# Cross-attention and mixture-of-experts kernel: the sums of squares move to two fp32r matmuls of parts that GpSimd makes, and the small work of each step is dealt out anew

## The chip, the core and the metric

One core of one Trainium2 chip runs the whole kernel in one launch. The metric is the device time of an execution in microseconds. Three executions of the kernel before are known; the median is what the change is measured against.

## What is computed

```python
x = x + xattn(layernorm(x), ctx, Wq, Wk, Wv)
x = x + moe(layernorm(x), Wr, br, gate_bias, Wup, ..., Wsd, bsd)

def xattn(x, context, Wq, Wk, Wv):            # 4 batches, 512 queries, 512 keys, 32 heads of 16
    q = rmsnorm((x @ Wq.T) per head)
    k = rmsnorm((context @ Wk_rows.T) per head)
    v = context @ Wv_rows.T
    return softmax(q @ k.T / 4) @ v
# rmsnorm(t) = t * rsqrt(mean(t * t, over the 16 of a head) + 1e-6)
```

The second part, a router with the best two of seven experts and one shared expert, all 512 wide, is not touched by the change.

## The kernel before

The attention part runs first, then `att.close()` gives its memory back and the experts follow. The attention work is cut into 16 units: a unit `u` is one batch `b` and one group `g` of 128 of the 512 columns, which holds 8 heads. A unit has 8 steps: `ab` (0 or 1) picks the even or the odd heads, `mt` one of four tiles of 128 keys. In a step `s`, TensorE makes the scores of four heads for 128 keys and 512 queries (`scored`, L253), in the four banks of `scores`; ScalarE takes the exponential of all 2048 columns at once (L610) into one of the two halves of `probs`; TensorE weighs the values with them (`weighed`, L270) and gathers the result in `o_ps`. There is one `scores`, so the next scores wait for the exponential, and the weighing of a step runs behind the scores of the next.

Between `scored` and `weighed` TensorE does everything else, in an order that is written out by hand in `between(u, s)` (L372): it projects k of the unit one or two ahead into `bank_a` (`k_chunk`, 3 matmuls each, four times a unit) and q of the unit two ahead into `bank_b` (`q_passes`, 4 matmuls each, three times a unit), sums the squares of q and k per head, turns the finished output (`out_transposes`), and in some groups computes the values of the next batch (`v_all`, twelve matmuls), transposes normalised rows (`norm_transposes`, `norm2_transposes`) and the router's logits (`gates`). All matmuls of projections are fp32r, three for one product: values are split into a high part, rounded to fp32r, and what is left.

The sums, transposes and logits go through one bank, `tr`; whose turn it is is fixed by the list in `uses` (L137), and each use waits on `tr_free` for the one before it to be read out. The sum of squares is a matmul with `blocks`, a matrix of ones in blocks of 16, so that each row gets the sum of its head:

```python
nc.scalar.activation(sq[:], bank_b[:], ACT.Square).then_inc(sqq_done, 1)                      # ScalarE, L483
nc.tensor.matmul(tr[:], blocks[:], sq[:], start=True, stop=True).then_inc(tr_ready, 1)        # TensorE, L329
```

It is plain fp32. The reciprocal root is made by ScalarE as exp(-0.5 ln(sum)) (`log_q`, `root_q`), and VectorE improves it by one Newton step, for which it needs the square of the root, `r2`, that ScalarE makes too (`root2_q`, `root2_k`, L518 and L523). `r0` and `r2` serve q and k in turn. Then VectorE copies each head's columns into the stacked form that the scores read (`stack_q`, `stack_k`), in high and low parts.

ScalarE's queue is written out in `before_exp(u, s)` (L536): what it does ahead of the exponential of a step. VectorE's is `step(u, s)` (L802). GpSimd has only seven small powers (`root`, L174) and a few memsets in this part. SyncE's queue has the loads. Each of these queues runs strictly in its written order.

The start, ahead of the loop, does the same for units 0 and 1, and the values of batch 0. Here the order of TensorE is k of unit 0, the transposes, k again, `sum_k(0)`, q of unit 0, the first values, `sum_q(0)` (L425 to L446); that of VectorE `sums_k(0)`, the low part of Wv (L929, 128x2048), `first_root_k(0)`, `newton_k(0)` and on.

## Time and profile before

| | |
|---|---|
| runs of the kernel before | 1047.79, 1046.66, 1047.68 us |
| median | 1047.68 us |
| the profiled execution | 1044.39 us, span of its profile 1042.7 us |
| granted TensorE clock over the span | 0.979 |
| TensorE matmul busy | 965.7 us (93%) |
| VectorE busy | 704.6 us (68%) |
| ScalarE busy | 517.6 us (50%) |
| GpSimd busy | 103.9 us (10%) |
| the 128 exponentials of the attention | from 41.40 to 480.90 us, 1878 ns each |

Times in the views are microseconds from the start of the span. PE is TensorE's matmuls, PEld its weight loads, DVE VectorE, ACT ScalarE, POOL GpSimd. The end of a matmul row is modelled and overlaps the next, so lengths of matmuls are read from start to start. An fp32 matmul of the program stands as two rows.

### The profile page before, as it was taken

The page shows a single profiled execution, that of the slowest core. Times are in us where ns is not written, and L with a number is a line of the kernel's source. Part 1 is how long each engine was busy: PE and PEld are TensorE (multiplying, and loading weights), DVE is VectorE, ACT ScalarE, POOL GpSimd, SP SyncE. Part 2 cuts the span into 40 slices and gives each one's busy share as a digit, 9 for nine tenths or more (in the row PEclk, how much of TensorE's full clock was granted, in tenths as well). Part 3 has the DMA queues.
Part 4 walks back from the last instruction along what each step waited for, and adds up shares of the span by engine and source line. Part 5 has one row for each costly group of instructions (what it writes and reads, how often), then busy time and mean ns, then how long its engine had stood idle before and what let it go on. Part 6 is the DMA issues. An engine that isn't in the chain of part 4 may idle for free.

```text
span 1042.7 us, 17880 instructions
## 1 busy us (share of the span) xinstructions
PE 965.7 (93%) x6728; PEld 692.5 (66%) x6729; DVE 704.6 (68%) x1387; ACT 517.6 (50%) x626; POOL 103.9 (10%) x135
## 2 busy tenths in 40 slices
PE   4999999989998999976999999999999999999686
PEld 3534443355344553332998989999899999999676
DVE  6787867876687667663678866575656574765288
ACT  4487768856786668875233232242424333342121
POOL 1000000000000000001000121111010101010652
PEclk9999999999999999997899999999999999999889
DMA  9400100001000100201410044124151542421654
GB/s 342 162 1 2 41 1 1 21 2 61 2 1 21 62 1 1 102 21 41 154 69 21 22 172 181 61 90 162 55 197 50 207 179 68 172 72 60 185 188 151
DMA packets 30024, 88.64 MB, mean 85 GB/s; under 512 B 5136, under 2 KB 5136, under 8 KB 25872
## 3 DMA queue, kind: packets, MB, share of 16 engines
q1 hardware_dynamic: 23088, 65.34, 17.0%
q0 software_dynamic: 6880, 22.55, 7.1%
q8 instruction: 36, 0.59, 0.2%
q14 instruction: 20, 0.16, 0.0%
HBM read 65.33 MB, written 22.54 MB: 84 GB/s over the span
## 4 chain that ended last, share of the span: by engine, by line
PE 45%; DVE 4%; another core or an unknown queue 2%; issue 1%; DMA 1%; ACT 1%; POOL 0%; POOLq 0%; DVEq 0%; ACTq 0%
PE u_ps L1178 14%; PE z_ps L1178 14%; PE y_ps L1178 13%; PE xt_ps L1191 2%; DVE x_sb L1611 1%; DMA xg<-xn_dram,index 1%; PE z_ps L1172 0%; DVE x_lo L1388 0%; DVE u_lo L1540 0%; PE xt_ps L1204 0%; DVE g_sb L1552 0%; DVE stats L1394 0%; DVE x_sb L1571 0%; ACT u_hi L1313 0%
## 5 line engine op out<-in xcount | busy, mean ns | idle before, releaser
L610 ACT ACTIVATE probs<-scores 128x2048 f32<-128x2048 f32 x128 | 240.4, 1878 | 78.0 <-PE scores L265 76.3
L1178 PE MATMUL z_ps<-u_hi,w_sb 128*128 128x256 f32 x896 | 167.2, 284 | 2.0 <-issue 1.9
L1178 PE MATMUL u_ps<-x_hi,w_sb 128*128 128x256 f32 x896 | 164.5, 282 | 4.0 <-issue 2.4
L1313 ACT ACTIVATE u_hi<-u_ps,b_ug 128x256 fp32r<-128x256 f32 x112 | 47.0, 471 | 237.1 <-PE u_ps L1178 235.1
L1178 PE MATMUL y_ps<-w_sb,g_hi 128*128 128x512 f32 x448 | 143.7, 402 | 12.2 <-DVE g_lo L1557 8.0
L1178 PEld LDWEIGHTS u_ps<-x_hi,w_sb 128*128 128x128 f32 x896 | 139.8, 189 | 6.9 <-issue 3.7
L1178 PEld LDWEIGHTS z_ps<-u_hi,w_sb 128*128 128x128 f32 x896 | 140.3, 189 | 2.8 <-issue 2.6
L281 PE MATMUL o_ps<-probs,v_sb 128*17 128x512 f32 x1024 | 137.3, 609 | 1.0 <-ACT probs L610 1.0
L1178 PE MATMUL z_ps<-u_lo,w_sb 128*128 128x256 f32 x448 | 126.1, 281 | 0.1
L1178 PE MATMUL u_ps<-x_lo,w_sb 128*128 128x256 f32 x448 | 125.7, 280 | 0.0
L265 PEld LDWEIGHTS scores<-q_st,k_hi 32*128 32x128 f32 x512 | 25.0, 183 | 124.0 <-ACT probs L610 70.5
L1540 DVE SCALAR_TENSOR_TENSOR u_lo<-u_ps,b_ug,u_hi 128x256 fp32r<-128x256 f32 x112 | 48.8, 478 | 84.1 <-ACT u_hi L1313 83.4
L1178 PEld LDWEIGHTS y_ps<-w_sb,g_hi 128*128 128x128 f32 x448 | 83.6, 192 | 31.7 <-DVE g_lo L1557 6.8
L1326 ACT ACTIVATE s_sb<-z_ps,b_ug 128x256 f32<-128x256 f32 x112 | 47.0, 470 | 112.3 <-PE z_ps L1178 93.8
L1178 PE MATMUL y_ps<-w_sb,g_lo 128*128 128x512 f32 x224 | 89.5, 400 | 0.0
L1552 DVE SCALAR_TENSOR_TENSOR g_sb<-u_ps,b_ug,s_sb 128x256 f32<-128x256 f32 x112 | 53.8, 481 | 50.4 <-ACT s_sb L1326 44.6
L1178 PEld LDWEIGHTS u_ps<-x_lo,w_sb 128*128 128x128 f32 x448 | 84.7, 189 | 1.0
L1178 PEld LDWEIGHTS z_ps<-u_lo,w_sb 128*128 128x128 f32 x448 | 85.1, 190 | 0.0
L265 PE MATMUL scores<-q_st,k_hi 32*128 32x512 f32 x512 | 64.9, 496 | 11.0 <-ACT probs L610 9.0
L1378 DVE TENSOR_TENSOR w_sb<-w_raw,w_sb 128x2048 fp32r<-128x2048 f32 x27 | 60.5, 2284 | 0.0
L1567 DVE TENSOR_TENSOR y_sb<-y_ps,bd 128x512 f32<-128x512 f32 x56 | 36.8, 686 | 27.0 <-PE y_ps L1178 16.3
L1301 ACT ACTIVATE w_sb<-w_raw 128x2048 fp32r<-128x2048 f32 x27 | 50.9, 1923 | 2.7 <-PEq L947 2.7
(206 smaller groups left out, 1488.9 us busy)
## 6 DMA issues: line engine op xcount, KB each, us to landing
w_raw<-w_all SPq DMA_DIRECT2D x27, 1024.0 KB, 8.6
y_dram<-y_sb SPq DMA_DIRECT2D x40, 256.0 KB, 2.1
ctx_raw<-ctx_t SPq DMA_DIRECT2D x4, 1024.0 KB, 6.1
out<-x_sb SPq DMA_DIRECT2D x16, 256.0 KB
y_dram<-xt SPq DMA_DIRECT2D x1, 3584.0 KB, 20.5
x_sb<-x SPq DMA_DIRECT2D x1, 3072.0 KB, 17.5
xn_dram<-xn SPq DMA_DIRECT2D x12, 256.0 KB, 2.0
bd<-b_down SPq DMA_DIRECT2D x9, 256.0 KB, 3.3
```

The costliest lines, as they stand in the source:

```text
L265: last = nc.tensor.matmul(scores[:, j, :], part[rows, u % 2, ab, mt * P:(mt + 1) * P], q_st[rows, u % 2, ab, :], start=(part is k_hi), sto ...
L281: last = nc.tensor.matmul(o_ps[32 * j:32 * j + HD + 1, :], v_sb[b % 2][:, mt, head, :], probs[:, t % 2, j, :], start=(mt == 0), stop=(mt = ...
L610: nc.scalar.activation(probs[:, t % 2], scores[:], ACT.Exp).then_inc(p_ready, 1)
L1178: ins = nc.tensor.matmul(out_ps, stat[a], mov[b], start=(first and a + b == 0), stop=(last and a == 1), skip_group_check=True)
L1191: last = nc.tensor.transpose(xt_ps[:, b, a, h * P:(h + 1) * P], xg[:, h, c * P:(c + 1) * P], ident[:])
L1301: nc.scalar.activation(w_sb[:, par, 0, m], w_raw[:, m], ACT.Copy).then_inc(hi_done, 1)
L1313: last = nc.scalar.activation(u_hi[:, c, :], u_ps[:, b, a, :], ACT.Identity, bias=b_ug[:, par, 0, c:c + 1])
L1326: nc.scalar.activation(s_sb[:, c, :], z_ps[:, b, a, :], ACT.Silu, bias=b_ug[:, par, 1, c:c + 1]).then_inc(s_done, 1)
L1378: nc.vector.tensor_tensor(w_sb[:, par, 1, m], w_raw[:, m], w_sb[:, par, 0, m].bitcast(FP32), ALU.subtract).then_inc(lo_done, 1)
L1540: nc.vector.scalar_tensor_tensor(u_lo[:, c, :], u_ps[:, b, a, :], bias[:, c:c + 1], u_hi[:, c, :].bitcast(FP32), ALU.add, ALU.subtract)\
L1552: nc.vector.scalar_tensor_tensor(g_sb[:, c, :], u_ps[:, b, a, :], bias[:, c:c + 1], s_sb[:, c, :], ALU.add, ALU.mult).then_inc(g_done, 1)
L1567: nc.vector.tensor_tensor(y_sb[:, h, :], y_v[:, h, :], bd[:, par, :], ALU.add).then_inc(y_done, 1)
```

## The change

Five things, all in the attention part:

- The sum of squares becomes two fp32r matmuls, of `sq_hi` and `sq_lo`, with a matrix of ones `blocks_r` that is fp32r as well. GpSimd makes the two parts from `sq`: a copy and a subtraction (`square_parts`). TensorE waits for `sq_split` instead of for ScalarE's square.
- GpSimd makes `r2` in place of ScalarE, as a product. Its order is written out as a loop over the units.
- The q and k matmuls are dealt out in fours and twos, one after the other, over the eight steps (`K_TURNS`, `Q_TURNS`; in units with an early block of values q has 4, 5 and 3 in three steps). `sum_k` goes from step 2 to step 3.
- Work that follows a read-out of `bank_a` (the second block of values, the first transposes of a batch, in group 1 the k matmuls of step 6) is issued behind `weighed`, in `after(u, s)`.
- ScalarE's small operations move: `log_k` from step 3 to 4, `root_k` from 4 to 5, `square_q` from 7 to 6; the second evacuation of transposed rows goes to VectorE (`norm_both(b + 1, 1)`). VectorE's statistics, `sums_k` and `first_root_k` move along. In the start `sum_k(0)` goes behind the q matmuls.

```diff
+            def square_parts(use):
+                n = SUM_AT[use]
+                pool.wait_ge(sqk_done if use[0] == "sum_k" else sqq_done, use[1] + 1)
+                if n:
+                    pool.wait_ge(tr_ready, TR_AT[SUMS[n - 1]] + 1)
+                nc.gpsimd.tensor_copy(sq_hi[:], sq[:]).then_inc(sq_high, 1)
+                pool.wait_ge(sq_high, n + 1)
+                nc.gpsimd.tensor_tensor(sq_lo[:], sq[:], sq_hi[:].bitcast(FP32), ALU.subtract).then_inc(sq_split, 1)
+
+            def root2_q(u):
+                pool.wait_ge(rq_ready, u + 1)
+                pool.wait_ge(norm_done, 2 * u if u else 1)
+                nc.gpsimd.tensor_tensor(r2[:], r0[:], r0[:], ALU.mult).then_inc(r2q_ready, 1)
...
+            square_parts(("sum_k", 0))
+            root2_k(0)
+            square_parts(("sum_q", 0))
+            root2_q(0)
+            square_parts(("sum_q", 1))
...
+        K_TURNS = {6: (0, 4), 7: (4, 6), 0: (6, 10), 1: (10, 12)}
+        Q_TURNS = {2: (0, 4), 3: (4, 6), 4: (6, 10), 5: (10, 12)}
+        Q_TURNS_V = {3: (0, 4), 4: (4, 9), 5: (9, 12)}
...
-            def sum_k(u):
-                begin("tr", TR_AT, ("sum_k", u), tr_free)
-                pe.wait_ge(sqk_done, u + 1)
-                nc.tensor.matmul(tr[:], blocks[:], sq[:], start=True, stop=True).then_inc(tr_ready, 1)
+            def sum_up(use):
+                begin("tr", TR_AT, use, tr_free)
+                pe.wait_ge(sq_split, SUM_AT[use] + 1)
+                nc.tensor.matmul(tr[:], blocks_r[:], sq_hi[:], start=True, stop=False, skip_group_check=True)
+                nc.tensor.matmul(tr[:], blocks_r[:], sq_lo[:], start=False, stop=True, skip_group_check=True)\
+                  .then_inc(tr_ready, 1)
...
-            k_chunk(0, 2)
-            k_chunk(0, 3)
-            sum_k(0)
-            for part in range(3):
-                q_passes(0, part)
+            k_turns(0, 6, 12)
+            q_turns(0, 0, 12)
+            sum_up(("sum_k", 0))
             v_all(scores[:, 0, :], 0, 0).then_inc(first_v, 1)
-            sum_q(0)
+            sum_up(("sum_q", 0))
...
                 elif s == 3:
-                    if nxt:
-                        root2_q(u + 1)
                     if more and g == 2:
                         norm_high(b + 1, 3)
+                elif s == 4:
                     if nxt:
                         log_k(u + 1)
-                elif s == 4:
+                elif s == 5:
                     if nxt:
                         root_k(u + 1)
-                elif s == 5:
                     group_out(u, 0)
                 elif s == 6:
                     if more and g == 1:
                         norm_high(b + 1, 0)
-                    if nxt:
-                        root2_k(u + 1)
-                else:
-                    if more and g == 1:
-                        norm_high(b + 1, 1)
                     if u + 2 < UNITS:
                         square_q(u + 2)
```

Where it shows, first in a plain unit on TensorE: unit 12's last step, which has a sum of q, and the step after it. A `scores` pair opens a step, `o_ps` closes it; `bank_a` rows are k matmuls, `tr` rows with `sq` the sum. Before:

```order
L288 MATMUL bank_a<-ctx_hi,wk_hi 128x512
L288 MATMUL bank_a<-ctx_lo,wk_hi 128x512
L288 MATMUL bank_a<-ctx_hi,wk_lo 128x512
L329 MATMUL tr<-sq,blocks 128x512
L281 MATMUL o_ps<-probs,v_sb 17x512 x4
L265 MATMUL scores<-q_st,k_hi 128x512 x4
L265 MATMUL scores<-q_st,k_lo 128x512 x4
L288 MATMUL bank_a<-ctx_hi,wk_hi 128x512
L288 MATMUL bank_a<-ctx_lo,wk_hi 128x512
L288 MATMUL bank_a<-ctx_hi,wk_lo 128x512
L281 MATMUL o_ps<-probs,v_sb 17x512 x4
```

and of the change:

```order
L369 MATMUL bank_a<-ctx_lo,wk_hi 128x512
L369 MATMUL bank_a<-ctx_hi,wk_lo 128x512
L387 MATMUL tr<-sq_hi,blocks_r 128x512
L388 MATMUL tr<-sq_lo,blocks_r 128x512
L336 MATMUL o_ps<-probs,v_sb 17x512 x4
L320 MATMUL scores<-q_st,k_hi 128x512 x4
L320 MATMUL scores<-q_st,k_lo 128x512 x4
L369 MATMUL bank_a<-ctx_hi,wk_hi 128x512
L369 MATMUL bank_a<-ctx_lo,wk_hi 128x512
L369 MATMUL bank_a<-ctx_hi,wk_lo 128x512
L369 MATMUL bank_a<-ctx_hi,wk_hi 128x512
L336 MATMUL o_ps<-probs,v_sb 17x512 x4
```

The step with the sum has two k matmuls beside it and no longer three, the next one four and no longer three.

Then the start, on TensorE, around the first sum. Before, with the end of unit 0's k matmuls ahead of it and the first q matmuls behind:

```order
L288 MATMUL bank_a<-ctx_lo,wk_hi 128x512
L288 MATMUL bank_a<-ctx_hi,wk_lo 128x512
L334 MATMUL tr<-sq,blocks 128x512
L300 MATMUL bank_b<-xt_hi,wq_hi 128x512
L300 MATMUL bank_b<-xt_lo,wq_hi 128x512
```

and of the change, with the last of the twelve q matmuls ahead of it and the first values behind:

```order
L356 MATMUL bank_b<-xt_hi,wq_hi 128x512
L356 MATMUL bank_b<-xt_lo,wq_hi 128x512
L356 MATMUL bank_b<-xt_hi,wq_lo 128x512
L387 MATMUL tr<-sq_hi,blocks_r 128x512
L388 MATMUL tr<-sq_lo,blocks_r 128x512
L343 MATMUL scores<-wv_hi,ctx_hi 128x512
```

The sum of k has moved past twelve q matmuls. On GpSimd the start and the first unit now read, where only the power and the memset stood:

```order
L192 TENSOR_TENSOR rsqrt<-mean_sq,power 128x4
L227 MEMSET xt 128x512
L211 CAST sq_hi<-sq 128x512
L213 TENSOR_TENSOR sq_lo<-sq,sq_hi 128x512
L224 TENSOR_TENSOR r<-r 128x512
L211 CAST sq_hi<-sq 128x512
L213 TENSOR_TENSOR sq_lo<-sq,sq_hi 128x512
L218 TENSOR_TENSOR r<-r 128x512
```

Parts of k, `r2` of k, parts of q, `r2` of q: this pattern of six operations repeats for every unit.

## Rows read from the trace of the kernel before

**Rows 1.** Units 10, 11, 12: length; PE, PEld, DVE, ACT, POOL busy; PEclk, DMA.
```profile
319.68:355.68 36.00, 32.54 (x221) 17.21 (x222) 25.89 (x51) 20.90 (x19) 0.00 (x0) 1.00 0.06 23
355.68:386.97 31.29, 31.16 (x213) 16.45 (x214) 18.57 (x37) 20.43 (x19) 0.00 (x0) 1.00 0.13 43
386.97:410.64 23.67, 23.19 (x165) 9.13 (x166) 16.11 (x33) 20.30 (x19) 0.00 (x0) 1.00 0.00 1
```

**Rows 2.** Timeline of ScalarE, unit 12 (start, duration, line, operation, idle before).
```profile
386.97 1.88 ACT L610 ACTIVATE probs<-scores 128x2048 f32<-128x2048 f32 x1 [0.15 <-PE scores L265]
...
389.34 0.64 ACT L512 ACTIVATE r<-r 128x512 f32<-128x512 f32 x1
389.87 1.87 ACT L610 ACTIVATE probs<-scores 128x2048 f32<-128x2048 f32 x1
391.63 0.59 ACT L489 ACTIVATE sq<-bank_a 128x512 f32<-128x512 f32 x1
...
392.67 1.88 ACT L610 ACTIVATE probs<-scores 128x2048 f32<-128x2048 f32 x1 [0.44 <-PE scores L265]
...
395.72 1.86 ACT L610 ACTIVATE probs<-scores 128x2048 f32<-128x2048 f32 x1
...
398.51 1.88 ACT L610 ACTIVATE probs<-scores 128x2048 f32<-128x2048 f32 x1 [0.42 <-PE scores L265]
...
401.30 1.88 ACT L610 ACTIVATE probs<-scores 128x2048 f32<-128x2048 f32 x1
...
404.51 1.88 ACT L610 ACTIVATE probs<-scores 128x2048 f32<-128x2048 f32 x1 [0.82 <-PE scores L265]
...
407.24 1.88 ACT L610 ACTIVATE probs<-scores 128x2048 f32<-128x2048 f32 x1 [0.36 <-PE scores L265]
...
410.64 1.88 ACT L610 ACTIVATE probs<-scores 128x2048 f32<-128x2048 f32 x1
```

**Rows 3.** Timeline of TensorE, last step of unit 11 and start of unit 12.
```profile
383.44 0.50 PE L288 MATMUL bank_a<-ctx_hi,wk_hi 128*128 128x512 f32 x1
...
384.24 1.02 PE L329 MATMUL tr<-sq,blocks 128*128 128x512 f32 x2
385.19 1.05 PE L281 MATMUL o_ps<-probs,v_sb 128*17 128x512 f32 x8
386.18 0.51 PE L265 MATMUL scores<-q_st,k_hi 32*128 32x512 f32 x4
...
386.84 0.50 PE L288 MATMUL bank_a<-ctx_hi,wk_hi 128*128 128x512 f32 x1
```

**Rows 4.** Timeline of VectorE, unit 11, after the second block of values.
```profile
379.24 0.69 DVE L729 COPY v_sb<-bank_a 128x512 f32<-128x512 f32 x1 [1.54 <-PE bank_a L288]
```

**Rows 5.** Timeline of TensorE, unit 10: two waits for the bank tr.
```profile
326.47 1.12 PE L334 MATMUL tr<-sq,blocks 128*128 128x512 f32 x2 [0.77 <-DVEq L797]
...
342.93 0.66 PE L340 MATMUL tr<-ident,o_sb 128*128 128x128 f32 x4 [1.81 <-DVE xt L714]
```

**Rows 6.** Groups of GpSimd, 0 to 500 us (count, busy, mean ns, idle).
```profile
L176 POOL TENSOR_TENSOR rsqrt<-mean_sq,power 128x4 f32<-128x4 f32 x7 | 7.4, 1062 | 404.3 <-DVE mean_sq L636 404.3
...
L188 POOL MEMSET xt<- 128x512 f32 x1 | 0.5, 519 | 0.0
...
L181 POOL TENSOR_SCALAR_AFFINE_SELECT blocks<-blocks 128x128 f32<-128x128 f32 x1 | 0.3, 343 | 0.1
```

**Rows 7.** Timeline of the start, VectorE, TensorE and ScalarE.
```profile
22.70 2.29 DVE L643 TENSOR_TENSOR wv_lo<-v_raw,wv_hi 128x2048 fp32r<-128x2048 f32 x1 [0.24 <-DVE ssk L741]
...
24.12 0.40 PE L300 MATMUL bank_b<-xt_hi,wq_lo 128*128 128x512 f32 x1
...
25.04 0.50 PE L288 MATMUL scores<-wv_hi,ctx_hi 128*128 128x512 f32 x1 [0.52 <-DVE wv_lo L643]
...
40.86 0.63 ACT L495 ACTIVATE r<-ssq 128x512 f32<-128x512 f32 x1 [3.07 <-DVEq L737]
```

**Rows 8.** 470 to 475 us, in unit 15, columns as in Rows 1.
```profile
470.00:475.00 5.00, 5.00 (x30) 2.64 (x30) 0.17 (x1) 2.25 (x3) 0.00 (x0) 0.57 0.00 0
```

More of the change, by code:

```diff
@@ new lines, in _ @@
+            roots = 1
+            for u in range(UNITS):
+                b, g, more, behind = batch_of(u)
+                if u + 1 < UNITS:
+                    root2_q(u + 1)
+                    square_parts(("sum_k", u + 1))
+                if behind and g == 1:
+                    root(roots, 1)
+                    roots += 1
+                if u + 1 < UNITS:
+                    root2_k(u + 1)
+                if u + 2 < UNITS:
+                    square_parts(("sum_q", u + 2))
+                if u == 1:
+                    pool.wait_ge(w_split, len(W_AT))
+                    nc.gpsimd.memset(v_sb[1][:, :, :, HD:], 1.0).then_inc(ones_set, 1)
+                if u == 0 or (g == GROUPS - 1 and b + 2 < BATCH):
+                    root(roots, 0)
+                    roots += 1
@@ L290, in three, with q_turns @@
                 return ins
-            def q_passes(u, part):
+            TURNS = [(c, a, b) for c in range(DC) for a, b in ((0, 0), (0, 1), (1, 0))]
+            def q_turns(u, first, end):
                 g = u % GROUPS
-                if part == 0:
+                if first == 0:
                     begin("b", B_AT, ("q", u), b_free)
@@ L297, in q_passes @@
                     pe.wait_ge(xt_split, (u // GROUPS + 1) * BT)
-                turns = [(c, a, b) for c in range(DC) for a, b in ((0, 0), (0, 1), (1, 0))]
-                for c, a, b in turns[4 * part:4 * part + 4]:
+                for c, a, b in TURNS[first:end]:
                     last = nc.tensor.matmul(bank_b[:], (wq_hi, wq_lo)[a][:, g, c, :], (xt_hi, xt_lo)[b][:, c, :],
@@ new lines, in between @@
+                if s == 1 and u:
+                    out_transposes(u - 1, 1)
+                if s == 2 and early_v:
+                    use = ("v", b + 1, 2 * g - 4) if u else ("v", 0, 2)
+                    begin("b", B_AT, use, b_free)
+                    v_all(bank_b[:], *use[1:]).then_inc(b_ready, 1)
+                if s == 2 and more and g == 2:
+                    norm_transposes(b + 1, 3)
+                if s == 3 and u + 1 < UNITS:
+                    sum_up(("sum_k", u + 1))
@@ new lines, in between, with after @@
+                if s == 7 and ahead:
+                    sum_up(("sum_q", u + 2))
+            def after(u, s):
+                b, g, more, behind = batch_of(u)
+                if s == 5:
+                    if more and g >= 2:
+                        begin("a", A_AT, ("v", b + 1, 2 * g - 3), a_free)
+                        v_all(bank_a[:], b + 1, 2 * g - 3).then_inc(a_ready, 1)
+                    if more and g == 1:
+                        norm_transposes(b + 1, 0)
+                if s == 6 and more and g == 1:
+                    k_turns(u + 2, *K_TURNS[s])
@@ L866, in step @@
                         context_split(b + 1, 3)
+                    stat1(3)
+                    if behind and g == 0:
+                        stat(tile_of(b - 1, 0), mv2[:, 0, :])
                 elif s == 5:
```

172 lines of the change are left out of this document (69 added, 103 removed).

## The prediction

> **What bounds the kernel now.** I read the times of each engine by stretch first, then the timeline of the attention loop, then the timeline of the start. The change lies wholly in the attention part: the 128 steps take from 41.40 to about 483 us of the 1042.7 us span, and everything behind runs the same instructions. In the stretches, three kinds of units are to be seen [rows 1]: unit 12, a plain one, takes 23.67 us with TensorE busy 23.19; unit 11, which also computes values for the next batch, 31.29 with 31.16; unit 10, which in addition splits the context and normalises, 36.00 with 32.54, and there VectorE is busy 25.89. GpSimd does nothing in any of them.
>
> The timeline shows the loop of one step: the exponential takes 1.88, the next scores can only start when it is over, and the one behind them starts about 0.79 after the scores did (386.18 to 386.97 [rows 2, 3]). The shortest step is 2.73 (404.51 to 407.24 [rows 2]). TensorE has in each step 0.66 of scores (386.18 to 386.84) and 0.99 of weighing (385.19 to 386.18 [rows 3]); what stands between them fits free of cost only up to some 1.1. Four fp32r matmuls fill it just: that step is 2.79 (398.51 to 401.30 [rows 2]), so they take 1.14, which I read as 0.23 each and 0.22 once. Four transposes on top make it 3.21 (to 404.51), 0.42 more. Three k matmuls and the sum of squares take 1.75 (383.44 to 385.19 [rows 3]), and 0.66 + 1.75 + 0.99 = 3.40 is the step that ends at 410.64 [rows 2]. So steps are uneven: some wait for ScalarE with TensorE idle, others run over, and the spare time of the first is lost.
>
> **The sums.** The fp32 sum adds 0.84 to its step (1.75 less the 0.91 of three matmuls alone). Two fp32r matmuls add 0.46. That is 0.38 less, twice a unit: 0.77.
>
> **The balance, plain unit (4, 8, 12, 13).** By the new rows of TensorE no step has more than four matmuls or two and the transposes: 2.79, or 2.79 - 0.46 + 0.42 = 2.75. The step ahead of the first exponential of a unit (two k, two of the sum) goes from 3.40 to 2.79. The next two: ScalarE's two operations ahead of one exponential still make 2.90 (386.97 to 389.87, the second is L512 [rows 2]), and 2.73 follows: 5.63 instead of 5.70. The third, which had the square of the root and the logarithm on ScalarE, goes from 3.05 (392.67 to 395.72) to 2.79, since only four q matmuls are left. The fourth stays at 2.79. The next two have again two operations in front of one exponential (root and copy): 5.63 for 6.00 (398.51 to 404.51). The last gets four k matmuls: 2.79 for 2.73. Sum 22.42 for 23.67: **1.25 saved, 5.0 in four units**.
>
> **Units with more in them.** Units 1, 5, 9 add two transposes; the evacuation of the second goes to VectorE (two operations of some 0.7), ahead of the k stack that the next unit waits for, and the bank tr is free later for sum_q. I take 0.8 each, 2.4. In units 3, 7, 11 TensorE is short in nearly every step [rows 1], so the balance brings nothing and the sums 0.77; against it, four k matmuls now stand directly behind the scores, where bank A is still read: the copy of the values takes 0.69 [rows 4] and starts as the scores start, and they wait about 0.3. With what balance is left I take 0.75 each, 2.3. Units 6 and 10: sum_k waited 0.77 for the bank [rows 5] and now finds the transposes ahead of it, so that wait falls behind twelve value matmuls; 0.77 + 0.77, less a new wait of norm2's transposes for sum_k's read-out, which stands behind VectorE's Newton step now: 1.4 each, 2.8. The wait of 1.81 at 342.93 [rows 5] is VectorE's own chain and stays. Unit 2 0.6, unit 14 0.4, unit 0 0.2, unit 15 nothing. Loop: 5.0 + 2.4 + 2.3 + 2.8 + 1.2 = **13.7 saved**.
>
> **GpSimd's parts.** Per unit it gets two copies, two subtractions and two products of 128x512, which no row shows. Below, none can cost less than the memset of that shape, 0.52; above, the affine select of 128x128 takes 0.34, so a one-input operation at most 1.36 and a two-input one twice that, 2.7 [rows 6]. I take 0.8 for a copy and 1.4 for a two-input operation: a part of the 0.34 is fixed, and the product of 4 columns at 1.06 is a power, which is nearer to the middle than to either end. Parts of one sum: 2.2, between 1.0 and 4.1. The deadline: square_k ends 0.34 after the scores of its step start (391.63 + 0.59, those start 0.79 ahead of 392.67 [rows 2]), and TensorE wants the parts 2.79 + 0.66 = 3.45 after them. With hops of 0.2, 2.9 is free; for sum_q, behind two k matmuls, 3.3. So 2.2 is hidden, and TensorE doesn't wait. The products replace two operations of 0.62 of ScalarE, of which the one in the third step was paid; they have two steps each.
>
> **What contention may cost.** GpSimd worked beside VectorE nowhere in this loop [rows 1], so nothing shows it: at best nothing, at worst each of some six operations holds VectorE for its whole length where VectorE sets the pace. I take 1.5 in all, for units 6 and 10 and the ends of units 1, 5, 9. The Trainium skill (SBUF — State Buffer, Who interferes with whom) says that a VectorE instruction with two SBUF inputs and a GpSimd one that reads SBUF exclude each other, whole instructions long; that speaks against this change, no run here shows it, and by it the sum would be that of the third rival below.
>
> **The start.** Here something is paid. sum_k(0) ran ahead of the twelve q matmuls and now stands behind them, and VectorE reads it before it makes the low part of Wv (L643, 2.29), which the first values wait for (they start at 25.04, right as it ends [rows 7]). Without the old sum ahead of them the q matmuls end at 24.35 - 0.84 = 23.5, the sum at 23.95, its read-out (0.7 and 0.15 of hop) at 24.8, Wv's part at 27.2, the values start at 27.3: 2.3 later. sum_q(0) then waits for GpSimd, which gets root, square and both parts late, about 0.8. The last sum comes late as well, and the first exponential stands behind its logarithm (40.86 [rows 7]): 0.4. **3.5 lost**, between 2.2 (only Wv) and 5.5 (all of GpSimd's waits).
>
> **Sum.** -13.7 + 1.5 + 3.5 = -8.7. The profiled execution took 1044.39 (span 1042.7 and 1.7 around it), so 1035.7 for such a one; the median of the three runs is 1047.68, 3.3 above, and against it I predict **1039.0**. What a measurement of this kernel can tell from no change is about 0.2%, 2.1 us.
>
> **Rivals.** (1) Slower: GpSimd's parts come too late for TensorE. With 4.1 for a pair TensorE waits 1.3 for each of 15 sum_k and 0.85 for each of 14 sum_q: 31, and at the start some 4 more: 1039.0 + 31 + 4 = 1074. It decides from about 3.4 for a pair: 0.5 x 15 + 0.1 x 14 = 8.9 eats the gain. For it: two-input work of this width is nowhere in the trace, and a 4-column product takes 1.06 [rows 6]. Against: that one is a power; the memset runs at VectorE's pace. 0.12.
> (2) The start costs nothing or little, because the first values had time: then 1035.5, and with no contention 1034. Against it is the row of 25.04, which starts on the very end of Wv's part. 0.13.
> (3) VectorE and GpSimd hold each other up. Of VectorE's 16.11 in a plain unit [rows 1] ten operations take two inputs from SBUF (four of Newton's steps, four that write the stacks, two additions), at some 0.69 [rows 4] 6.9, and GpSimd would read for 7.2 (two copies, four two-input operations); together 14.1 of 22.4, so plain units have room, but in units 6 and 10 and where a logarithm waits for VectorE (once a unit) some 0.4 a unit is lost, 6.0 instead of 1.5: 1043.5, and with a start of 5.5 1045.5, within 0.2% in the end. For it: VectorE is the pace of unit 10. 0.15.
> (4) TensorE's clock. It was at 0.57 of full speed in unit 15 [rows 8], the lower of its two levels for most of these 5 us, after steps with only scores and weighing; that costs about 2.5. With less to do in units 14 and 15, and with idle time at the start, it may fall once more or once less: 1036.5 or 1041.5. 0.05, and part of the range.
>
> **How the numbers follow.** Forecast 0.55. Its own range is 1036 to 1042. For 8 in 10 I go down to 1033 (rival 2 and a clock that stays up) and up to 1046.5 (rival 3), and leave out rival 1 and the tails. Faster by over 0.2% (below 1045.6): the forecast, rivals 2 and 4 and a part of 3, 0.79. Within 0.2%: the rest of 3 and a mild form of 1, 0.10. Slower: rival 1, 0.11.
>
> **What would show it.** Plain units near 22.4 from exponential to exponential, none of their steps above 2.95; sum rows of 0.46 spacing; the first exponential near 45 instead of 41.40, with the values' start after Wv's part at 27.3. GpSimd's subtraction at about 1.4 and its copy at 0.8. Wrong is the step on GpSimd if TensorE's sums have idle time in front of them released by GpSimd in plain units; wrong is the one on contention if VectorE's two-input operations get longer than 0.69 to 0.75 or GpSimd's vary between calls of one shape; wrong is the start if the first values begin before 26.

## The result and the profile after

The changed kernel takes **1059.95 us** (median of 4 runs, 1058.51 to 1061.40) against 1047.74 for the kernel before on the same chip (4 runs): a ratio of 1.0109, interval 1.0088 to 1.0131. It is slower by 12.2; the prediction was 1039.0, range 1033.0 to 1046.5. Its profiled execution took 1059.17, span 1057.2.

The head of the page of the changed kernel with each engine's busy time, share and instructions:

```profile
span 1057.2 us, 17971 instructions
...
PE 961.9 (91%) x6728; PEld 698.1 (66%) x6729; DVE 734.4 (69%) x1390; ACT 497.1 (47%) x591; POOL 208.0 (20%) x232
```

The attention loop from the first exponential to the last, of before and of after (columns as in [rows 1]):

```profile
41.40:480.90 439.50, 416.18 (x2897) 188.31 (x2901) 304.69 (x608) 322.69 (x286) 6.71 (x7) 0.99 0.06 20
```
```profile
48.29:493.50 445.21, 408.10 (x2899) 188.48 (x2901) 332.15 (x611) 303.00 (x253) 103.71 (x95) 0.99 0.06 20
```

TensorE did 8.1 less, as meant, and the loop still took 5.7 more. VectorE was busy 27.5 longer, with three more operations (611 for 608; in e7 below the same 611 take 307.01, so 2.3 of it is theirs and 25.1 is not), while GpSimd worked 97 more than before. The first exponential came 6.9 later. What lies behind the last one took 561.8 before and 563.7 after, with the same instructions; in e1 to e6 and e8 below it lay between 560.1 and 562.9 whatever was changed, so I don't count this part as the change's.

Units 10, 11, 12, which answer to [rows 1]:

```profile
335.24:371.42 36.18, 31.89 (x220) 16.63 (x219) 27.51 (x51) 19.98 (x19) 6.19 (x6) 1.00 0.06 23
371.42:402.92 31.50, 30.86 (x213) 16.44 (x214) 18.51 (x36) 19.30 (x17) 5.94 (x6) 1.00 0.13 43
402.92:427.06 24.14, 23.73 (x172) 9.86 (x176) 18.21 (x35) 18.99 (x16) 7.25 (x6) 1.00 0.00 1
```

Unit 12 was to fall from 23.67 to 22.42 and rose to 24.14. The steps inside it are as forecast to within 0.25; the one that leads into unit 13 took 4.38 instead of 2.79. Here is that step, the one in front of unit 13's first exponential, first VectorE:

```profile
420.04 0.98 DVE L783 TENSOR_TENSOR r<-ssk,r 128x512 f32<-128x512 f32 x1
421.05 1.65 DVE L784 SCALAR_TENSOR_TENSOR kn<-r,kn 128x512 f32<-128x512 f32 x1
...
424.04 0.75 DVE L816 SCALAR_TENSOR_TENSOR k_lo<-twin,sign,k_hi 128x512 fp32r<-128x512 f32 x1
424.70 0.69 DVE L661 BATCH_NORM_STATS2 stats<-x_sb 128x6 f32<-128x512 f32 x1
425.43 0.18 DVE L662 BATCH_NORM_AGGREGATE mv<-stats 128x2 f32<-128x6 f32 x1
425.64 0.69 DVE L764 TENSOR_SCALAR ssq<-tr 128x512 f32<-128x512 f32 x1
```

GpSimd and ScalarE in the same stretch:

```profile
419.59 0.89 POOL L211 CAST sq_hi<-sq 128x512 fp32r<-128x512 f32 x1 [1.43 <-ACT sq L532]
420.55 1.60 POOL L213 TENSOR_TENSOR sq_lo<-sq,sq_hi 128x512 fp32r<-128x512 f32 x1
```
```profile
426.52 0.63 ACT L544 ACTIVATE r<-ssq 128x512 f32<-128x512 f32 x1 [1.96 <-DVEq L766]
427.06 1.86 ACT L639 ACTIVATE probs<-scores 128x2048 f32<-128x2048 f32 x1
```

`kn` at L784 takes 0.69 when alone. Here it takes 1.65 and ends at 422.70, 0.55 after GpSimd's subtraction (420.55 + 1.60 = 422.15): it ended as if it had begun its work only when GpSimd was through. "Holding" below means this: a row of VectorE (or of GpSimd) that is longer than the same instruction alone, because it waits for the other engine to finish. Behind it on VectorE stand the k stack, the statistics (0.69 and 0.18) and only then the reading of the sum (L764), for which ScalarE's logarithm waited 1.96 with the exponential behind it.

The largest single loss is the seventh step of unit 2, 11.04 where before had 5.97. (A step is counted by the exponential that it ends in: the first step of a unit leads to its first exponential.) VectorE, GpSimd and TensorE:

```profile
122.03 0.83 DVE L689 CAST ctx_hi<-ctx_raw 128x512 fp32r<-128x512 f32 x1
122.89 1.63 DVE L681 TENSOR_TENSOR ctx_lo<-ctx_raw,ctx_hi 128x512 fp32r<-128x512 f32 x1
124.45 0.68 DVE L780 TENSOR_TENSOR kn<-bank_a,r 128x512 f32<-128x512 f32 x1
```
```profile
121.91 0.67 POOL L211 CAST sq_hi<-sq 128x512 fp32r<-128x512 f32 x1 [1.93 <-ACT sq L532]
122.66 1.32 POOL L213 TENSOR_TENSOR sq_lo<-sq,sq_hi 128x512 fp32r<-128x512 f32 x1
```
```profile
125.18 0.50 PE L343 MATMUL bank_a<-wv_hi,ctx_hi 128*128 128x512 f32 x1 [3.44 <-DVE kn L780]
...
127.31 0.63 PE L343 MATMUL bank_a<-wv_hi,ctx_hi 128*128 128x512 f32 x1
127.73 0.63 PE L343 MATMUL bank_a<-wv_lo,ctx_hi 128*128 128x512 f32 x1
```

The second block of values needs bank A, which `first_root_k` (L780) still has to read, and that stands behind two context tiles (again `ctx_lo` ends 0.54 after GpSimd). TensorE waits 3.44, and then its granted clock is at the lower of its two levels, so that the matmuls follow each other by 0.43 instead of 0.23:

```profile
123.00:126.00 3.00, 0.82 (x3) 0.67 (x4) 2.82 (x5) 0.00 (x0) 0.98 (x1) 0.99 0.21 30
126.00:129.00 3.00, 3.00 (x8) 2.31 (x7) 0.32 (x1) 0.00 (x0) 0.00 (x0) 0.50 0.79 320
```

In the kernel before, `first_root_k` of this unit ran at 110.80, 1.2 ahead of the sixth exponential (112.00); in the changed one 5.0 behind it (119.48). ScalarE's logarithm and root moved a step later, and VectorE's reading went with them, behind the context.

The start answers to [rows 7]:

```profile
25.85 0.39 PE L388 MATMUL tr<-sq_lo,blocks_r 128*128 128x512 f32 x1
29.56 0.50 PE L343 MATMUL scores<-wv_hi,ctx_hi 128*128 128x512 f32 x1 [3.32 <-DVE wv_lo L672]
```

### The profile page after: what moved, and what is told of

Read it like the earlier page. It is cut to its first block, busy times and chain, and to the rows that moved or that the text cites. A ratio compares the mean times of both kernels' runs of the same rounds, so it can differ in the third digit from the quotient of the medians.

```text
span 1057.2 us, 17971 instructions
## 1 busy us (share of the span) xinstructions
PE 961.9 (91%) x6728; PEld 698.1 (66%) x6729; DVE 734.4 (69%) x1390; ACT 497.1 (47%) x591; POOL 208.0 (20%) x232
## 4 chain that ended last, share of the span: by engine, by line
PE 46%; DVE 3%; issue 2%; another core or an unknown queue 1%; ACT 1%; ACTq 0%; DVEq 0%
PE u_ps L1207 15%; PE y_ps L1207 14%; PE z_ps L1207 13%; PE xt_ps L1220 2%; PE z_ps L1201 1%; DVE x_sb L1640 0%; PE xt_ps L1233 0%; ACT u_hi L1342 0%; DVE u_lo L1569 0%; DVE stats L1423 0%; DVE hot_row L1534 0%; ACT s_sb L1355 0%; DVE x_lo L1417 0%; DVE g_sb L1581 0%
## 5 line engine op out<-in xcount | busy, mean ns | idle before, releaser
L1136 POOL COPY index<-table 128x2 int32 (+1 forms) x23 | 4.4, 192 | 329.2 <-PE xt_ps L1220 295.0
```

## The experiments

All times are in us, those of a step or a loop from the profiled execution; "loop" is from the first exponential to the last (before 439.5, after 445.2). e1 to e4 ran together, so did e5 to e8, e9 to e12, and e13 with e14; each ratio is against the kernel before in the same series (its medians: 1044.78, 1048.09, 1032.06, 1045.10), and times of different series are not compared with each other. Two theories at first: A, the order on VectorE decides; B, VectorE and GpSimd hold each other. Theory C comes with e9.

**e1: the start in the order of before, without GpSimd** (`sum_old` is the fp32 matmul of before; the third sum and the squares of the roots likewise).

```diff
             k_turns(0, 6, 12)
+            sum_old(("sum_k", 0), sqk_done)
             q_turns(0, 0, 12)
-            sum_up(("sum_k", 0))
             v_all(scores[:, 0, :], 0, 0).then_inc(first_v, 1)
-            sum_up(("sum_q", 0))
+            sum_old(("sum_q", 0), sqq_done)
...
-            square_parts(("sum_k", 0))
-            root2_k(0)
-            square_parts(("sum_q", 0))
-            root2_q(0)
-            square_parts(("sum_q", 1))
```


> Only the start is as in the kernel before: fp32 sums of the squares, sum_k(0) ahead of the q matmuls, the two squares of the roots on ScalarE; the loop is the changed one. Theory A (the place of sum_k(0) and the parts on the way of the first values cost the start): the first exponential starts between 41.5 and 43.5 instead of 48.29, the first values near 25 to 26.5 instead of 29.5, and the time falls by 4.5 to 6.5 from the changed kernel's. Rival (the loads came later in that execution, the order costs only the 2.3 of the low part of Wv): the first exponential at 44 to 46, 2 to 3.5 less.

1050.9, ratio 1.0067 (1.0045 to 1.0088). First exponential at 41.28 instead of 48.29, loop unchanged (445.8). By the two ratios the start is 0.42% or 4.4 of the 12.2; each ratio has an interval of 0.2% to either side, so this alone is 4.4 give or take 3. The trace is sharper: from the last matmul of k's first projection (19.42) to the first exponential it is 21.86 again, where the kernel before has 21.89.

**e2: context tiles 2 and 3 of a g 2 unit behind `finalize`.**

```diff
-                    if more and g == 2:
-                        context_split(b + 1, 2)
-                        context_split(b + 1, 3)
                     stat1(3)
...
                     finalize(u, 0)
+                    if more and g == 2:
+                        context_split(b + 1, 2)
+                        context_split(b + 1, 3)
```


> VectorE's two last context splits stand behind the read-out of bank A (first_root_k) and the first output, no longer ahead of them. Theory A (the order on VectorE decides: the second block of values waits for first_root_k): in unit 2 the step of 11.04 falls to 5.7 to 6.5 and the clock stays at full there; units 6 and 10 lose 1 to 2 each; in all 7 to 9 less. Theory B (GpSimd holding VectorE up decides, wherever first_root_k stands): the values still wait 2 or more and the clock still falls, 0 to 3 less.

1047.9, ratio 1.0024 (1.0009 to 1.0039); loop 438.8. The seventh step of unit 2 falls from 11.04 to 5.97, those of units 6 and 10 from 8.3 to 6.15. With GpSimd at work, the order was worth 6.4 in the loop. Not all of this repairs the change: units 6 and 10 had 8.0 in this step already in the kernel before, with these tiles in front of the copy that TensorE waited 1.81 for [rows 5]. The holding only moved: it now falls on a copy with one input.

```profile
122.68 1.40 DVE L689 CAST ctx_hi<-ctx_raw 128x512 fp32r<-128x512 f32 x1
```

**e3: the statistics of a g 0 unit behind the read-out of the next sum.**

```diff
-                    if behind and g == 0:
-                        stat(tile_of(b - 1, 1), mv2[:, 1, :])
...
                         stack_k(u + 1, 1)
+                    if behind and g == 0:
+                        stat(tile_of(b - 1, 1), mv2[:, 1, :])
```


> The statistics of one tile move on VectorE from in front of sums_q to behind it, in the units of group 0 (4, 8, 12). Theory A (order): the first exponential of units 5, 9, 13 comes 0.9 earlier, 4.40 becomes 3.5, in all 2.7 less. Theory B (GpSimd's subtraction makes the Newton step 0.95 longer in just this chain): the same 0.9 goes, but 0.7 above the 2.8 of the other units stays, so 3.5 and not 2.8. Rival (the wait is TensorE's): 4.4 stays.

1055.26, ratio 1.0104 (1.0065 to 1.0143); loop 444.65. The first step of units 5, 9, 13 falls from 4.40 to 3.44, 0.96 each, and stays 0.6 above the 2.8 of the others, as theory B had it. In units 5 and 9 half of the gain comes back in the seventh step (3.69 to 4.11). Alone it can't be told from the changed kernel.

**e4: GpSimd's subtraction replaced by two memsets.** The low part of the squares is zero, so it is left out of the sums. GpSimd writes twice and reads nothing there.

```diff
-                nc.gpsimd.tensor_tensor(sq_lo[:], sq[:], sq_hi[:].bitcast(FP32), ALU.subtract).then_inc(sq_split, 1)
+                nc.gpsimd.memset(sq_lo[:].bitcast(FP32), 0.0).then_inc(spare_done, 1)
+                pool.wait_ge(spare_done, n + 1)
+                nc.gpsimd.memset(sq_lo[:].bitcast(FP32), 0.0).then_inc(sq_split, 1)
```


> GpSimd's subtraction is replaced by two memsets of the same tensor, 0.52 each: GpSimd reads nothing in that time. It leaves out the low part of the squares (zero in its place). TensorE, its waits and the orders are as in the changed kernel. Theory B (reads of GpSimd and of VectorE exclude each other): VectorE's second Newton operation on k (L784, 1127 ns in the mean, 1.65 where it overlaps) falls to 0.7 to 0.8, the first exponential of units 5, 9, 13 comes 0.9 earlier, the wait in unit 2 gets 1 to 1.5 shorter, in all 5 to 8 less. Theory A (order alone): the operations stay as long as they are, within 1 of the changed kernel.

1048.53, ratio 1.0043 (1.0014 to 1.0073); loop 438.8, the same 6 shorter as e2 with VectorE's order untouched. The group of `kn` on VectorE and of the two memsets on GpSimd, which together take 1.08:

```profile
L786 DVE SCALAR_TENSOR_TENSOR kn<-r,kn 128x512 f32<-128x512 f32 x15 | 10.7, 711 | 0.5
```
```profile
L213 POOL MEMSET sq_lo<- 128x512 f32 x29 | 15.6, 538 | 1.7
```

`kn` was 1098 in the changed kernel: there seven of the 15 lie under GpSimd's copy or subtraction and are longer, six of them 1.65 or 1.66 and one 0.98; the other eight take 0.69. Here a memset lies over part of six of them, and those take 0.69. A GpSimd that only writes doesn't hold it; the one row that is longer, 0.98, lies under GpSimd's copy, which reads. Steps that A gives to the order alone (the first of units 2, 6, 10) fell from 5.69 to 4.73.

**e5: the changed kernel again**, so that e6 to e8 have their zero.

> The changed kernel as it is, on the chip of the runs beside it, so that they have their own zero. Every theory: 1.011 times before, about 1056; first exponential near 48.3, loop near 445.

1058.49, ratio 1.0103 (1.0076 to 1.0130); first exponential 46.39, loop 444.9.

**e6: the squares of the roots back on ScalarE.**

```diff
-                nc.gpsimd.tensor_tensor(r2[:], r0[:], r0[:], ALU.mult).then_inc(r2q_ready, 1)
...
+                nc.scalar.activation(r2[:], r0[:], ACT.Square).then_inc(r2q_ready, 1)
```


> The squares of the roots go back to ScalarE, at the steps where they stood before; GpSimd keeps the parts of the squares. Theory B (VectorE and GpSimd hold each other): GpSimd's two products of 1.04 to 1.88 a unit are gone, newton_k in units 5, 9, 13 gets shorter and the start loses 2 (0.62 instead of 1.88, twice): about 1052 to 1053. Theory A (only the order on VectorE decides): the loop pays up to 0.2 a unit for the two operations of ScalarE and gains nothing: start -1.5, loop +3, about 1058.

1057.79, ratio 1.0092 (1.0066 to 1.0118): as A had it, but not for its reason. Unit 2 took 30.72 instead of 34.08, and `q_st` 752 ns instead of 866. Units 4, 5, 8, 9 and 12 lost 0.3 to 0.5 each, and units 10 and 14 took 2.4 and 2.0 more: in each of these TensorE waited 1.72 and 1.42 for VectorE, and then its clock fell. The sum is nothing.

```profile
325.55 0.50 PE L371 MATMUL tr<-sq_hi,blocks_r 128*128 128x512 f32 x1 [1.72 <-DVEq L737]
```
```profile
327.00:330.00 3.00, 2.44 (x14) 1.36 (x11) 2.66 (x6) 1.45 (x2) 0.00 (x0) 0.52 0.03 5
330.00:333.00 3.00, 3.00 (x15) 1.36 (x13) 2.58 (x5) 1.01 (x1) 0.00 (x0) 0.50 0.19 70
```

**e7: nothing of the norms on GpSimd.** Beside e6, ScalarE writes the squares straight into `sq_hi` and both matmuls read it; the sums come out about twice as large, and the low part is left out. The gates then get other numbers, and what lies behind the loop (547, with 17541 instructions in all instead of 17971) is not to be compared. The loop has the same 611 operations of VectorE and the same matmuls.

```diff
-                nc.scalar.activation(sq[:], bank_b[:], ACT.Square).then_inc(sqq_done, 1)
+                nc.scalar.activation(sq_hi[:], bank_b[:], ACT.Square).then_inc(sqq_done, 1)
...
-                nc.tensor.matmul(tr[:], blocks_r[:], sq_lo[:], start=False, stop=True, skip_group_check=True)\
+                nc.tensor.matmul(tr[:], blocks_r[:], sq_hi[:], start=False, stop=True, skip_group_check=True)\
```


> GpSimd does nothing for the norms: ScalarE writes the squares rounded to fp32r straight into the high part's tile, both matmuls of a sum read that tile, and the squares of the roots are ScalarE's again. The low part of the squares is left out of the sums. TensorE's and VectorE's instructions are those of the changed kernel. Theory B: all the holding is gone, VectorE's kn is back at 0.69 and x_sb at 0.43, the first step of units 5, 9, 13 falls from 4.40 to 2.8 to 3.4, those of units 6 and 10 from 5.69 to about 4.5, the first exponential comes 3 earlier; unit 2's step 6 stays above 9, because the order there is the same: about 1044. Theory A: the order is unchanged, so the loop gains at most 2 and the start 2: about 1052.

The loop and the group of `kn`:

```profile
45.45:478.34 432.89, 405.12 (x2896) 187.08 (x2900) 307.01 (x611) 318.87 (x283) 7.58 (x7) 1.00 0.06 20
```
```profile
L779 DVE SCALAR_TENSOR_TENSOR kn<-r,kn 128x512 f32<-128x512 f32 x15 | 10.4, 692 | 0.5
```

432.9 against 444.9 of e5: **the loop is 12.0 shorter without GpSimd's work**, and VectorE's busy time is back from 332 to 307. Some 11 of it is the holding; 1.1 is a fall of TensorE's clock in unit 15 that e5 has and e7 hasn't. Theory A allowed 2. Theory B was too strong in two places: it had unit 2's seventh step stay above 9 and the first exponential come 3 earlier, and it came 0.9 earlier (45.45 for 46.39). The whole took 1027.09, of which 13 less than e5 up to the last exponential (478.34 for 491.32) and the rest is the shorter part behind it. Unit 2's seventh step is 7.75: the order alone costs 1.8 there, the rest of the 5.1 needed the holding.

**e8: the edits of e1, e2 and e3 together.**

> The three edits of order of e1 to e3 together, with GpSimd's work as in the changed kernel. Theory A: their gains add up (5.3, 8.3 and 1): about 1042, faster than before by 0.25%. Theory B: the holds move to whatever VectorE does in those places, so a third is lost again: about 1046 to 1047, equal to before.

1044.3, ratio 0.9957 (0.9940 to 0.9974), a little faster than the kernel before; loop 437.5. Of the 7.5 less in the loop (against e5) 3.5 are unit 2, 1.8 unit 6 and 3.0 units 4, 8 and 12; unit 10 got back only 0.6, for TensorE's clock was at 0.56 from 353 to 356 us. The first step of units 2, 6, 10 stayed at 5.7 to 6.1.

**e9: the balance alone.** One fp32 sum as before, roots' squares on ScalarE, GpSimd nothing, start as before. What is left of the change is the distribution of the k and q matmuls, `sum_k` in step 3, the work behind `weighed`, ScalarE's small operations in their new steps, and with them VectorE's order and its second evacuation; no run takes these apart.

```diff
-                pe.wait_ge(sq_split, SUM_AT[use] + 1)
-                nc.tensor.matmul(tr[:], blocks_r[:], sq_hi[:], start=True, stop=False, skip_group_check=True)
-                nc.tensor.matmul(tr[:], blocks_r[:], sq_lo[:], start=False, stop=True, skip_group_check=True)\
-                  .then_inc(tr_ready, 1)
+                pe.wait_ge(sqk_done if use[0] == "sum_k" else sqq_done, use[1] + 1)
+                nc.tensor.matmul(tr[:], blocks[:], sq[:], start=True, stop=True).then_inc(tr_ready, 1)
```


> Only one part of the change: TensorE's new distribution of the k and q matmuls and ScalarE's logarithm and root in their new steps. The sums are one fp32 matmul as before, at the place in the step where the two fp32r ones stand; the squares of the roots are on ScalarE; the start is in the order of before; GpSimd has nothing of it. Theory A (my sum: balance worth 13.7 less the sums' 0.77 a unit in 14 units, about 3 to 5 in all): faster than before by 4 to 6, about 1042. Theory C (e7's loop of 432.9, that is 6.6 less than before's, is all that balance and sums are worth together without any holding): an fp32 sum costs 0.2 to 0.38 each more than the two, 29 of them 5 to 11, and nothing is left: 1047 to 1051, equal to before or slower.

1033.85 against 1032.06 of before on that chip, ratio 1.0023 (1.0007 to 1.0038): theory C. The loop is that of before to 0.4:

```profile
42.95:482.04 439.09, 415.75 (x2896) 186.31 (x2900) 306.84 (x611) 319.25 (x284) 7.59 (x7) 1.00 0.06 20
```

**The balance brings nothing as a whole**, and in these two executions it costs where the clock is left out: the kernel before lost time to a lower clock in unit 0 (0.57 from 44 to 48 us) and in unit 15 [rows 8], and e9 in neither, so units 1 to 14 took 393.5 in e9 where before had 389.8. Unit 14 took 2.0 more, with e9's clock at 0.57 from 456 to 460 us, unit 2 1.3 and unit 7 1.1. Units in us, first exponential to the next unit's:

| unit | before | e9, balance | e7, balance and short sums | e5, with GpSimd | forecast |
|---|---|---|---|---|---|
| 2 | 29.78 | 31.08 | 30.80 | 34.08 | 29.2 |
| 4, 8, 12 | 23.67 | 23.3 | 23.34 | 24.2 | 22.42 |
| 5, 9 | 25.73 | 25.95 | 25.3 | 26.27 | 24.9 |
| 7 | 31.93 | 33.07 | 32.69 | 32.74 | 31.2 |
| 10 | 36.00 | 35.44 | 35.10 | 36.15 | 34.6 |
| 11 | 31.29 | 32.06 | 31.46 | 31.44 | 30.5 |
| 13 | 23.68 | 23.24 | 22.18 | 22.17 | 22.42 |
| loop | 439.5 | 439.1 | 432.9 | 444.9 | 425.8 |

**e10: e9 with the late context and statistics of e2 and e3.**

> As e9, and the context splits of a g 2 unit and the statistics of a g 0 unit come later on VectorE, as in e2 and e3. By the theory of the order: unit 2's step 6 falls from 7.7 to 6.0, those of units 6 and 10 from 7.6 to 6.1, 4 to 5 less than e9. By the theory of the holding alone: nothing or 1, since no GpSimd operation holds VectorE here.

1031.9, ratio 0.9995 (0.9979 to 1.0010); loop 435.6, 3.5 less than e9. The seventh step went to 5.93 in all three g 2 units (from 7.29 in unit 2 and 7.6 in 6 and 10), without any GpSimd: the order costs by itself.

**e11: e8 with the high half of the second transposed block on ScalarE.**

```diff
-                        norm_both(b + 1, 1)
...
+                    if more and g == 1:
+                        norm_low(b + 1, 1)
...
+                    if more and g == 1:
+                        norm_high(b + 1, 1)
```


> As e8, and ScalarE again makes the high half of the second block of transposed rows in the g 1 units, one step later, as before; VectorE makes its low half. VectorE has one operation of 0.7 less ahead of stack_k: the first step of units 2, 6, 10 falls from 5.7 to about 4.9 and the whole by 2 to 3: 1042. Rival: ScalarE's copy delays an exponential by 0.1 to 0.2 and VectorE's chain is bound by its Newton step instead: 1044, equal to e8.

1032.81, ratio 1.0007 (0.9989 to 1.0025): a miss. The first step of units 2, 6, 10 rose to 7.25, 6.60, 5.83. In unit 1 the low half now stands behind the first k stack (it starts at 92.43), and it is what frees the bank for the sum, which VectorE reads at 94.48; the exponential follows at 97.08. Moving this copy to VectorE was right in the change.

**e12: e8 with the squares of the roots on ScalarE in the loop.**

> As e8, and the squares of the roots in the loop are ScalarE's, at their places of before; GpSimd keeps the parts. Theory B: q_st falls from 922 to 752 ns and x_sb to about 0.45, the first step of units 2, 6 and 10 by 0.3, but the first of units 5, 9, 13 rises as it did in e6 (4.87 for 4.39), because the logarithm there comes later: 1043 to 1045. Theory A: 1045.

1030.63, ratio 0.9982 (0.9968 to 0.9995); loop 438.7. `q_st` fell to 751 and the first step of units 5, 9, 13 rose to 3.9, both as theory B had it; the first of units 2, 6, 10 stayed at 5.9 to 6.1, which it hadn't. As in e6, one step each of units 10 and 14 was longer by 2.6 and 2.0, behind waits of 1.71 and 1.42 and at a lower clock.

**e13: e8 with GpSimd idle where VectorE's chain sets the pace. e14: e8 again, its zero.**

```diff
+        WHOLE = [("sum_k", u + 1) for u in range(UNITS) if batch_of(u)[1:3] == (2, True)]
+        WHOLE += [("sum_q", u + 2) for u in range(UNITS) if batch_of(u)[1] in (1, 2) and batch_of(u)[2]]
...
+                if use in WHOLE:
+                    pe.wait_ge(sqk_done if use[0] == "sum_k" else sqq_done, use[1] + 1)
+                    nc.tensor.matmul(tr[:], blocks_r[:].bitcast(FP32), sq[:], start=True, stop=True).then_inc(tr_ready, 1)
+                    return
...
+                    if not (more and g == 2):
+                        root2_q(u + 1)
```


> As e8, but GpSimd does nothing while VectorE's chain sets the pace: the sum of k of units 3, 7, 11 and the sums of q of units 3, 4, 7, 8, 11, 12 are one fp32 matmul of the square, and the squares of the roots during units 2, 6, 10 are ScalarE's; in the other units parts and roots stay on GpSimd. Theory B, that the holding costs only there: units 2, 6, 10 take 31.0, 35.1, 35.1 as in e10 instead of 33.9, 37.0, 38.4, the other units stay at e8's times, and the whole is 7 to 8 shorter than e8, 1.2% below before. Rival: the holding of the other units (q_st 922, kn 1099 ns) costs as well or moves, and the two kinds of sums get into each other's way: 2 or 3 shorter than e8.

> e8 once more, on the chip of e13: 0.996 of before, as in e8; the difference to e13 is what GpSimd's work in the g 2 units costs.

e13: **1036.69, ratio 0.9914 (0.9885 to 0.9943)**; e14: 1041.72, ratio 0.9958 (0.9936 to 0.9981). The loop:

```profile
42.69:473.50 430.81, 408.08 (x2896) 187.00 (x2900) 323.95 (x611) 306.27 (x260) 76.65 (x71) 1.00 0.06 21
```

The same row of e14 is 434.93 long with VectorE busy 332.60 and GpSimd 104.13. Counted by the steps that end in them, as the expectation does, units 2, 6, 10 take 31.2, 35.3 and 35.3 instead of 33.0, 37.0 and 38.4: 6.5 less (1.4 of it a clock of 0.54 in unit 10 of e14), and within 0.3 of the times of e10, which has no work of GpSimd. The fp32 sums gave about 1 back in units 3, 11 and 13, and a fall of the clock in unit 15 another 1, so the loop is shorter by 4.1 and the whole by 5.0, between the 7 to 8 of theory B and the 2 or 3 of its rival. In the other units nothing changed, though `q_st` is still 875 ns over the loop: VectorE is held in many places and pays in few. Units 2, 6, 10 aren't the only such place: ahead of the first exponential of units 5 and 9 `kn` still takes 1.65, and that step 3.45 where 3.17 was reached with an fp32 sum (e10); the seventh of unit 3 takes 6.49 instead of 5.93. No run takes GpSimd out of these alone. e13 is the best version: 0.9% shorter than the kernel before, against which the changed one was 1.0 to 1.1% longer. Not much of that is the change's own gain. The loop is 8.7 shorter than before's; 4.5 of it are units 6 and 10 (33.8 for 36.0), which take as little in e10 by the later tiles of e2, and 2.8 are units 0 and 15, where the kernel before had the lower clock for longer.

## Why the prediction was wrong

By its own steps, with the forecast first.

Two terms failed: contention, which turned the gain into a loss, and the balance.

**Contention, 1.5: the first step that failed.** It measured 12.0 in the loop (e5 444.9, e7 432.9; 11 without the fall of the clock in unit 15), seven to eight times the term. The prediction gave this outcome to rival 3 with 0.15 and priced it at 6.0 in all. Two things were wrong in its working. It counted VectorE's operations in a plain unit and found room (14.1 of 22.4); but what counts is the one instruction that stands ahead of a late one. `kn` at L784 meets the subtraction in the first step after every g 0 unit (4.39 against 3.58 in e7) and every g 1 unit (5.70 against 4.51). And it allowed "its whole length" of 1.4 only for six operations, where the profile has VectorE busy 25.1 longer over the loop for the same 611 operations (332.15 against 307.01 in e7). Four groups of VectorE in the changed kernel:

```profile
L808 DVE SCALAR_TENSOR_TENSOR q_st<-twin,lower,twin_hi 128x512 fp32r<-128x512 f32 x30 | 26.0, 866 | 1.1
...
L829 DVE TENSOR_TENSOR x_sb<-x_sb,o_n 128x256 f32<-128x256 f32 x30 | 16.9, 562 | 4.4 <-DVE o_n L824 0.2
L784 DVE SCALAR_TENSOR_TENSOR kn<-r,kn 128x512 f32<-128x512 f32 x15 | 16.5, 1098 | 0.5
...
L780 DVE TENSOR_TENSOR kn<-bank_a,r 128x512 f32<-128x512 f32 x15 | 10.3, 684 | 0.2
```

The first three were 751, 425 and 692 before; the last, which takes one of its inputs from PSUM, was 682 and is untouched. The Trainium skill (SBUF — State Buffer, Who interferes with whom) says just this: a VectorE instruction with two SBUF inputs and a GpSimd one that reads SBUF exclude each other for the whole instruction, one with a single SBUF input does not unless it is in a two-port mode. The runs agree where GpSimd works on 512 columns: e4's memset, which reads nothing, leaves `kn` at 711, `kn` from PSUM isn't longer, and the one-input copy that was held for 1.40 in e2 is one that takes 0.42 alone, where a copy out of PSUM takes 0.69 [rows 4]. They don't show it for the power of four columns, which reads too: it lies over the whole of three of the `kn` in the changed kernel (at 71.53, 160.77 and 280.11), and these take 0.69; the power takes 1.35 instead of 1.06. The prediction cited the rule and then took the row of before, which showed nothing for lack of any overlap, as nearer to "little" than to the rule.

**The balance, -13.7 with the short sums: the second step that failed.** Measured -6.6 without GpSimd (e7 against before), and even that is flattered: 2.6 of it are unit 15 and 1.2 unit 0, where the kernel before had the lower clock. Units 1 to 14, for which 13.5 was forecast, gained 2.8. The sums are right: 0.36 a step against 0.38 forecast (3.17 in e9, 2.81 with two fp32r matmuls), and so is the one plain unit with nothing else beside it (unit 13: 22.18 for 22.42). Units 4, 8, 12 were to gain 1.25 each and gained 0.3, with one fp32 sum as with two short ones (e9 23.3, e7 23.34). The step behind them, to the next unit's first exponential (3.2 in e9, 3.58 in e7), waits for VectorE: in e7 ScalarE stands idle for 1.18 until VectorE has read the sum, and only then makes the logarithm (410.85). The prediction priced TensorE and ScalarE there and not VectorE's queue. What failed besides is "0.8 each", "0.75 each" and "1.4 each" for the units with more in them. With fp32 sums (e9) the balance gained 0.4 in each plain unit, and lost 0.2 in units 5 and 9, 0.8 in unit 11 and 1.1 in unit 7. In unit 11 TensorE is busy 31.16 of 31.29 [rows 1], so I read this as work that leaves one long step and makes another longer; no run tests it. Units 3, 7 and 11 were to gain 0.75 each; in e7 unit 3 gained 0.3, and 7 and 11 lost 0.8 and 0.2. Units 6 and 10 gained 0.9 for 1.4. Units 1, 5 and 9 were to gain 0.8 and, even without GpSimd, gained 0.4 in two and nothing in unit 1.

**Unit 2, -0.6: wrong by 4.9.** The prediction moved ScalarE's logarithm and root of k a step later and charged ScalarE alone. VectorE's `first_root_k` went with them, fell behind two context tiles, and it is what frees bank A for the second block of values. That wait was named nowhere. It cost 1.3 in e9, 3.4 of idle TensorE with the holding on top, and about 1.6 more by the lower clock behind it (eight matmuls 0.43 apart instead of 0.23). Units 6 and 10 lost only 0.3 in that step, because the two tiles stood in a bad place there already: in front of the copy that frees `tr` for the output's transposes. TensorE waited 1.81 for it before [rows 5] and waits 2.14 in the changed kernel, as the prediction said it would stay:

```profile
358.73 0.66 PE L395 MATMUL tr<-ident,o_sb 128*128 128x128 f32 x4 [2.14 <-DVE xt L743]
```

Undoing the order (e2) gave 3.6 in unit 2 and 3.9 in units 6 and 10, and 6.4 in the loop; taking GpSimd's work away instead (e7) gave 3.3 in unit 2.

**The start, 3.5 (2.2 to 5.5): right in kind, short by 1.** From the last matmul of k's first projection to the first exponential it took 21.89 before (19.51 to 41.40) and 26.28 after (22.01 to 48.29), 26.68 in e5: 4.4 to 4.8. The order without GpSimd (e7: 20.38 to 45.45) costs 3.2 of it, GpSimd 1.2 to 1.6; the old start (e1) has 21.86. The first values started right on the end of Wv's low part, as forecast, but TensorE had idled 3.32 ahead of them. The other 2.5 of the 6.9 came ahead of that, where the two kernels run the same instructions: in this execution the first k matmul started at 15.45 instead of 13.80, in e5, which is the same kernel, at 14.05, and there the first k projection ended at 19.71. So it varies between executions.

**GpSimd's parts, 2.2 (0.8 and 1.4): right.** The copy took 0.61 alone and 0.69 in the mean, the subtraction 1.30 and 1.46, the product 1.04 and up to 1.88. Rival 1 was out: TensorE waits for the parts nowhere in the loop, and only once in the start (1.74 at 46.04). That they were in time was no comfort; who else they stopped was the question.

**Rival 4, the clock**, was in the range with one fall more or less, 2.5. Unit 15 went from 22.53 to 19.95 because its fall didn't come, which was luck for the forecast; unit 2 got one instead, and in unit 0 both kernels have one.

Put together: -13.7 became -6.6 by the balance and a kinder clock, +1.5 became +12.0 (of which a part is unit 2's order, that the holding made worse), and +3.5 became 4.6. That makes 10.0 against 12.2 between the medians. The remaining 2.2 are not assigned; the interval of the ratio is as wide (1.0088 to 1.0131, 2.3 to either side). e1's ratio puts the start at 4.4 and its loop, 445.8 against 439.5, at 6.3, which leaves 1.5 open; a fall of the clock in one unit moves a loop by 1 to 2.6, and no run separates the rest.

## What to carry to other kernels

Moving elementwise work to an idle GpSimd is not free when VectorE has two-input SBUF operations beside it. Price each as whole instructions added to the one VectorE instruction that is late in that step, and leave GpSimd idle where VectorE's chain sets the pace (that took the loop from 434.9 in e14 to 430.8 in e13, and the whole by 5.0). Count the steps by what they wait for and not by TensorE's work: matmuls moved out of a step gain nothing when that step ends in a wait for VectorE. And when a small operation moves a step later, follow its reader: on which engine does that stand, behind what, and which bank does it free.

## What was not expected of the hardware

A wait of TensorE can cost more than its length. After 3.44 idle (unit 2), 1.72 and 1.42 (e6) the granted clock was 0.50 to 0.56 of full speed for the next 3 to 6 us, which is the lower of its two levels, and the step behind took up to 2.6 longer. It needn't: after waits of 1.73 (e7, unit 2, at 118.25) and 1.69 (e6, unit 2) the matmuls followed each other by 0.23 as before, so the length of the one wait doesn't tell. And the holding goes both ways: VectorE's Wv part (27.21 to 29.50) made GpSimd's product of 1.04 last 1.88:

```profile
28.53 1.88 POOL L224 TENSOR_TENSOR r<-r 128x512 f32<-128x512 f32 x1 [3.43 <-ACT r L565]
```
